# First channel attention of a six-stage kernel: band added by halves of 64 rows, rows normed in place and kept on chip, loads moved

## What is computed

```python
x = _layernorm(x + _L0_attn_ref(x, ...), axis=-1)
x = _layernorm(x + _L0_xattn_ref(x, ctx_2048, ..., 64), axis=-1)
x = _layernorm(x + _L0_ffn_ref(x, ...), axis=-1)
...
def _L0_xattn_ref(mask, encodings, w_in, b_in, w_out, b_out, w_ct, b_ct, local_size):
    N, E, T, H = (8, 64, 256, 8)
    ...
    scores = jnp.einsum('bqhd,bkhd->bhqk', q, k) / jnp.sqrt(jnp.asarray(d, q.dtype))
    idx = jnp.arange(t)
    band = jnp.abs(idx[:, None] - idx[None, :]) <= local_size
    scores = jnp.where(band[None, None], scores, neg)
    attn = jax.nn.softmax(scores, axis=-1)
    o = jnp.einsum('bhqk,bkhd->bqhd', attn, v).reshape(n, t, e)
    ...
    y = jax.nn.relu(o) * encodings
    out = jnp.einsum('nit,io->not', y, w_ct) + b_ct[None, :, None]
```

## Time and profile before

| | |
|---|---|
| median of 3 runs | 3762.48 us (3760.27 to 3763.68) |
| the profiled execution | 3755.11 us |
| its span | 3753.3 us |
| mean granted TensorE clock | 0.945 of full speed |
| TensorE busy | 3290.9 us, 88% |
| VectorE, ScalarE, POOL busy | 65%, 51%, 52% |
| stage_banded | about 384 to 725 us of the span |
| MLP | about 728 to 925 us |

### The profile page before, as it was taken

The page is one execution under the profiler, slowest core; times in us unless marked ns, Lnnn a source line. Parts: engine busy times, 40 slices in busy tenths (PEclk is TensorE's granted clock), DMA queues, the critical chain, the costliest instruction groups (busy, mean ns, idle before and its releaser), DMA issues. The chain is left out here.

```text
span 3753.3 us, 100900 instructions
## 1 busy us (share of the span) xinstructions
PE 3290.9 (88%) x37352; PEld 2245.7 (60%) x37352; DVE 2431.1 (65%) x4462; ACT 1923.2 (51%) x5120; POOL 1968.1 (52%) x2814
## 2 busy tenths in 40 slices
PE   9999599786899999999999999999998398779990
PEld 6777366464566666666666666666666255446550
DVE  5555366333677777777777777777777378534446
ACT  1111255422566666666666666666665177545550
POOL 2333333142556665665565655665565357657772
PEclk9999799897999999999999999999999599989995
DMA  2000544200221111111111111111110256366645
GB/s 80 11 11 8 132 115 115 70 1 18 56 57 49 40 47 47 48 40 49 46 49 40 52 45 50 44 53 37 57 56 23 65 144 175 113 209 208 213 155 208
DMA packets 229331, 285.18 MB, mean 76 GB/s; under 512 B 58756, under 2 KB 193352, under 8 KB 222184
## 3 DMA queue, kind: packets, MB, share of 16 engines
q1 hardware_dynamic: 210440, 243.87, 23.0%
q0 software_dynamic: 18432, 34.96, 2.7%
HBM read 166.39 MB, written 127.93 MB: 78 GB/s over the span
## 5 line engine op out<-in xcount | busy, mean ns | idle before, releaser
L2090 PE MATMUL head_ring<-gd_xT,head_w 128*128 128x512 f32 x1024 | 520.9, 633 | 15.4 <-DMA head_w<-gd_w 10.0
L2519 POOL TENSOR_TENSOR head_V<-head_V,gd_ones 128x512 bf16<-128x512 f32 x128 | 133.3, 1041 | 476.2 <-DVE head_V L2373 476.2
L1386 POOL DMA_INDIRECT ytok<-exp_y,exp_cur x256 | 252.5, 986 | 121.4 <-issue 72.7
L2348 DVE SCALAR_TENSOR_TENSOR head_cb_V<-head_ring,head_taps,head_cb_V 128x504 f32<-128x504 f32 (+2 forms) x384 | 279.8, 729 | 13.0 <-ACT head_cb_V L2233 8.4
L2090 PEld LDWEIGHTS head_ring<-gd_xT,head_w 128*128 128x128 f32 x1024 | 181.9, 198 | 154.6 <-issue 131.6
L2209 PE MATMUL head_by<-head_wo,head_ogT 128*128 128x256 f32 x1024 | 255.5, 393 | 9.4 <-issue 6.1
L2379 DVE TENSOR_TENSOR head_Xs<-head_bx,head_join 128x512 bf16<-128x512 f32 x320 | 219.8, 687 | 62.3 <-PE head_bx L2131 55.9
L2099 PE MATMUL head_ring<-head_w,gd_xT 128*128 128x256 f32 x1024 | 257.3, 394 | 2.8 <-DVE head_cb_V L2348 2.4
L2270 ACT CAST head_Tt<-head_btt 128x512 bf16<-128x512 f32 x320 | 191.3, 598 | 38.1 <-PE head_btt L2139 36.7
L2209 PEld LDWEIGHTS head_by<-head_wo,head_ogT 128*128 128x128 f32 x1024 | 185.1, 190 | 39.4 <-issue 14.4
L2099 PEld LDWEIGHTS head_ring<-head_w,gd_xT 128*128 128x128 f32 x1024 | 185.3, 191 | 35.5 <-DVE head_cb_V L2348 3.4
(11 more groups left out here) (345 smaller groups left out, 9064.3 us busy)
## 6 DMA issues: line engine op xcount, KB each, us to landing
xbuf<-head_blank SPq DMA_DIRECT2D x64, 552.0 KB
exp_xg<-xbuf SPq DMA_DIRECT2D x64, 552.0 KB, 5.2
head_gi<-scan SPq DMA_DIRECT2D x64, 256.0 KB
ytok<-head_blank SPq DMA_DIRECT2D x64, 256.0 KB
sum_yg<-ytok SPq DMA_DIRECT2D x16, 1024.0 KB, 7.0
moe_w<-moe_w SPq DMA_DIRECT2D x32, 384.0 KB, 3.2
cb_Q<-qd SPq DMA_DIRECT2D x48, 192.0 KB
cb_K<-kd SPq DMA_DIRECT2D x48, 192.0 KB
```

The costliest lines, as they stand in the source:

```text
L1386: pool.indirect_dma_start(ytok, bass.IndirectOffsetOnAxis(ap=cur[i % AHEAD][s][:, b:b + 1], axis=0), y[i % RESULTS][s][:, b, :], None, bou ...
L2090: last = pe.matmul(b[:, :], w[:, c, FEAT[what]], xT[:, c, n % UNITS * N:n % UNITS * N + N], start=c == 0, stop=c == DC - 1)
L2348: dve.scalar_tensor_tensor(out=out, in0=by_seq(bank_of(f, n))[:, :, 0:SEQ - s], scalar=taps[:, TAP[f], KS - 1 - s:KS - s], in1=out, op0=AL ...
```

## The change

- The band is added by four products in place of one: for each query block and each half of 64 rows, the two blocks of 64 keys where the band is not zero, from the identity's diagonal quarter. Blocks of the band that are wholly 0 are left out.
- The rows and ctxt of the stage live in `xc`, which is now made before the stage. The norm is written back over x in `xc`; `y`, the stores to x2, x2 itself and the MLP's loads of x are gone. The load of ctxt in the delta stage is gone too, with its semaphore.
- The identity is loaded once, into a tile that lives until the delta stage ends. The MLP's mixing and gate weights, gamma and offset are loaded during the channel attention, one at each of fetches 6 to 9, into tiles that are given back before the heads of the delta stage.
- Tile 2 of x and ctxt is loaded at the start of the stage; tiles 1 and 2 now stand ahead of the constants.
- On POOL the casts of the identity and the band come before `prefill()`, which moves behind the split of tile 1.

```diff
+            def bounds(pe, bank):
+                for i in range(QB):
+                    for side in range(2):
+                        rows = slice(side * SEQ, side * SEQ + SEQ)
+                        into, held = (t[rows, i * KW:i * KW + KW].rearrange("p (c k) -> p c k", k=SEQ) for t in (bank, band16))
+                        chunks = slice(1 - i, 3 - i) if side == i else slice(0, 3, 2)
+                        pe.matmul(into[:, chunks, :], ident16[rows, rows], held[:, chunks, :], start=i == 0, stop=False, skip_group_check=True)
...
-                        pe.matmul(b[:, 0:QB * KW], ident16[:, :], band16[:, :], start=True, stop=False, skip_group_check=True)
+                        bounds(pe, b)
...
-                        pe.matmul(b[:, 0:KB * KW], ident16[:, :], band16[:, :], start=True, stop=False, skip_group_check=True)
+                        bounds(pe, b)
...
                 load(0)
                 for t, name in early:
                     sp.dma_start(t, A[name]).then_inc(early_in, 16)
+                load(1)
+                load(2)
                 for t, name in loads:
                     sp.dma_start(t, A[name]).then_inc(weights_in, 16)
-                load(1)
...
-                        for ahead in range(2 if t == 0 else t + 3, min(t + 4, TILES)):
-                            load(ahead)
+                        if t + 3 < TILES:
+                            load(t + 3)
+                        if t >= 6 and t - 6 < len(early_weights):
+                            to, name = early_weights[t - 6]
+                            sp.dma_start(to, name).then_inc(next_in, 16)
...
-                        sp.dma_start(dst[t * P:t * P + P, :], y[u][:, :]).then_inc(stored[u], 16)
-                for u in range(2):
-                    sp.wait_ge(stored[u], START + TILES // 2 * 16)
+                sp.wait_ge(next_in, START + 16 * len(early_weights))
...
-                        if n >= 2:
-                            dve.wait_ge(stored[u], START + n // 2 * 16)
-                        norm_apply(dve, ln[u], [y[u][:, :]], [r[u][:, :]], [mv[u][:, :]], [rstd[u][:, :]], n // 2, 1)
+                        norm_apply(dve, ln[u], [x[:, n, :]], [r[u][:, :]], [mv[u][:, :]], [rstd[u][:, :]], n // 2, 1)
...
-                    pool.wait_ge(weights_in, START + 16 * len(loads))
-                    pool.tensor_copy(ident16[:, :], ident[:, :]).then_inc(bits_ready, 1)
-                    pool.tensor_copy(band16[:, :], band[:, :]).then_inc(bits_ready, 1)
...
                         if n == 0:
+                            pool.wait_ge(weights_in, START + 16 * len(loads))
+                            pool.tensor_copy(ident16[:, :], ident[:, :]).then_inc(bits_ready, 1)
+                            pool.tensor_copy(band16[:, :], band[:, :]).then_inc(bits_ready, 1)
+                        elif n == 1:
                             prefill()
...
-                    sp.dma_start(ident[:, :], A["ident"]).then_inc(weights_in, 16)
-                    load(0)
-                    sp.dma_start(wm[:, :, 0:D], A["expert_w"].rearrange("(c p) e -> p c e", p=P)).then_inc(mixed_in, 16)
-                    sp.dma_start(wm[:, :, D:D + E], A["mlp_gate"].rearrange("(c p) e -> p c e", p=P)).then_inc(mixed_in, 16)
                     sp.dma_start(wup[:, :, :], A["up_w"].rearrange("(c p) e -> p c e", p=P)).then_inc(up_in, 16)
-                    load(1)
                     sp.dma_start(wdown[:, :, :], A["down_w"].rearrange("(c p) e -> p c e", p=P)).then_inc(down_in, 16)
-                    sp.dma_start(offset[:, :], A["ln_beta"]).then_inc(offset_in, 16)
-                    sp.dma_start(gamma[:, :], A["ln_gamma"]).then_inc(gamma_in, 16)
-                    for s in range(2, UNITS):
-                        load(s)
...
-                    sp.dma_start(xc[:, :, 1, :], ctxt.rearrange("(t p) d -> p t d", p=P)).then_inc(ctxt_in, 16)
```

More of the change, by code:

```diff
@@ L1467, in _, with __init__, loads, rows @@
                         norm_rstd(pool, ln[u], [mv[u][:, :]], [var[u][:, :]], eps[:, :], power[:, :], [rstd[u][:, :]], t // SLOTS, 1)
-def stage_delta(nc, src, ctxt, xc, scan, xbuf, ytok, A):
+class MlpWeights:
+    def __init__(self, m):
+        self.wm = m.sb("wm", [P, DC, D + 8])
+        self.gamma, self.offset = m.sb("gamma", [P, D]), m.sb("offset", [P, D])
+    def loads(self, A):
+        def rows(name):
+            return A[name].rearrange("(c p) e -> p c e", p=P)
+        return [(self.wm[:, :, 0:D], rows("expert_w")), (self.wm[:, :, D:D + 8], rows("mlp_gate")),
+                (self.gamma[:, :], A["ln_gamma"]), (self.offset[:, :], A["ln_beta"])]
+class DeltaState:
+    def __init__(self, m):
+        self.ident, self.ones = m.sb("ident", [P, P]), m.sb("ones", [P, P])
+        self.power, self.root, self.eps, self.eps6 = (m.sb(n, [P, 1]) for n in ("power", "root", "eps", "eps6"))
+        self.shrink, self.per_dim, self.minus1 = m.sb("shrink", [P, 1]), m.sb("per_dim", [P, 1]), m.sb("minus1", [P, 1])
+        self.xT = m.sb("xT", [P, DC, ROWS])
+        self.beta, self.gsum = m.sb("beta", [P, TILES, 32]), m.sb("gsum", [P, TILES, 32])
+def stage_delta(nc, xc, state, weights, weights_held, scan, xbuf, ytok, A):
     NK, NV, DH, KS = 16, 32, P, 4
@@ L1510, in stage_delta @@
             IC, PAIR, HALF = I // P, range(2), TS // 2
-            wm, wup, wdown = m.sb("wm", [P, DC, D + E]), m.sb("wup", [P, DC, I]), m.sb("wdown", [P, IC, D])
-            gamma, offset = m.sb("gamma", [P, D]), m.sb("offset", [P, D])
+            wm, gamma, offset = weights.wm, weights.gamma, weights.offset
+            wup, wdown = m.sb("wup", [P, DC, I]), m.sb("wdown", [P, IC, D])
             wab, upto = m.sb("wab", [P, DC, 2 * NV]), m.sb("upto", [P, P])
             dt, alog, rate = (m.sb(n, [P, NV]) for n in ("dt", "alog", "rate"))
-            x = [m.sb(f"x{s}", [P, TS, D]) for s in range(UNITS)]
+            x = [xc[:, s * TS:s * TS + TS, 0, :] for s in range(UNITS)]
             xb, moe = ([m.sb(f"{n}{u}", [P, TS, D]) for u in PAIR] for n in ("xb", "moe"))
@@ L2648, in build @@
     stage_lightning(nc, x[0], x[1], A)
-    stage_banded(nc, x[1], x[2], A["ctxt"], qd, kd, A)
     with ExitStack() as ctx:
-        xc = Mem(nc, ctx, "rows").sb("xc", [P, TILES, 2, D])
-        stage_delta(nc, x[2], A["ctxt"], xc, scan, xbuf, ytok, A)
+        rows = Mem(nc, ctx, "rows")
+        xc = rows.sb("xc", [P, TILES, 2, D])
+        with ExitStack() as delta:
+            state = DeltaState(Mem(nc, delta, "gd"))
+            weights_held = delta.enter_context(ExitStack())
+            weights = MlpWeights(Mem(nc, weights_held, "ahead"))
+            stage_banded(nc, x[1], A["ctxt"], xc, state.ident, qd, kd, A, weights.loads(A))
+            stage_delta(nc, xc, state, weights, weights_held, scan, xbuf, ytok, A)
         stage_moe(nc, xc, out, qd, kd, xbuf, ytok, A)
```

42 lines of the change are left out of this document (13 added, 29 removed).

## The result

The changed kernel takes 3839.5 us (median of four runs, 3836.99 to 3877.0) against 3761.4 for the kernel before (four runs, 3756.88 to 3763.68). The ratio is 1.0232, with a 95% interval of 1.0169 to 1.0296. The kernel is slower by 78 us by the medians and by 87 us by the ratio, in which the one long execution of 3877.0 us counts; +51.5 was forecast, with 3840 us (+77.5) as the end of the range. The ratio lies beyond that end (1.0206), though its interval reaches over it. Where the executions of one kernel lie more than 1.5% apart, ratios here use the shorter ones alone. The profiled execution, the shortest of the four, took 3836.99 us; its span is 3835.2.

A forecast was written before the change was run, and what follows sets the result against it. The prediction took TensorE's queue to bound the middle of the channel attention, so each unit's added cost shows 1 to 1. Halves +71, start -10 and seam -9.5 gave +51.5 us, 3814 us in all, range 3790 to 3840.

The forecast's parts named there:

- Part 1, the price of a block: Band products in the channel attention: a block by halves takes 0.33 us against 0.167, +0.163 us a unit.
- Part 1, the full clock: Middle of the channel attention: all 456 blocks costed at full clock, +74.3 us; sum of the part +71 us.
- The clock: Rival: many gaps lower the granted clock in the channel attention, some 30 us more, 3845 us; chance 0.07.
- Part 2, the start: Start of the channel attention: third tile's earlier load brings the second pass near 428 instead of 438.4, -10 us.
- its first half: Start of the channel attention: the first unit can start at about 408.5 us, 10 us earlier.
- The rival that the start gains nothing: Start of the channel attention: transfers of the first two tiles set it, +10, 3824 us; no chance of its own.
- Part 3, the seam: From channel attention to MLP: without the last store and reload, the first up-product comes near 735.5 instead of 744.84, -9.5 us.
- The sum: Whole kernel: 71 - 10 - 9.5 = +51.5 us, added to the median of 3762.5, gives 3814 us.

The follow-up runs named there:

- four_full: The changed kernel with the band added by four products of 96 columns on the full array: 3891.52 against 3910.68 us for the kernel before, ratio 0.9951.
- two_blocks_together: The changed kernel with the first pass's blocks of two units issued one behind the other: 3944.02 against 3901.18 us for the kernel before, ratio 1.0108.
- after_again: The changed kernel, unaltered, run again on a chip of the experiments: 3974 to 4026 us in four runs, ratio 1.0206 to the kernel before.
- whole_at_start: The changed kernel with whole products in the first 100 blocks and halves from there on: 3950.9 against 3910.68 us for the kernel before, ratio 1.0106.
- one_product: The changed kernel with the band added by one product of 384 columns again: 3892.24 against 3910.68 us for the kernel before, ratio 0.9944.
- place_first: The changed kernel with one product for the band and the spreads three steps later: 3886.69 against 3901.18 us for the kernel before, ratio 0.9959.
- one_third_late: The changed kernel with one product for the band and the third tile's load in its old place: 3880.65 against 3901.18 us for the kernel before, ratio 0.9957.
- late_and_place: The changed kernel with one product, the third tile's load in its old place and spreads three steps later: 3889.04 against 3907.89 us for the kernel before, ratio 0.9955.
- before_again: The kernel before, unaltered, profiled again on a chip of the experiments: 3898.08 us in its profiled execution.
- one_pair: The changed kernel with only two of each block's four products: 4022.0 to 4139.7 us, ratio 1.034 to the kernel before by the two shorter runs.

## Why the prediction was wrong

**Part 1, the price of a block: right.** 0.24 and 0.26 us between the starts, 22.85 us a tile against 22.7, 61 to 63 us for 412 blocks against 62. That the price is the change of shape is shown from both sides: four products without one cost 0.007 us a block (four_full), and taking two of a pair's four changes away gives 0.21 us of the expected 0.22 (two_blocks_together). Both agree with what the Trainium skill states (TensorEngine Tiling, Key Properties), that changing the tiling mode, not just the tile, drains TensorE; its price here is 0.09 us.

**Part 1, the full clock: this step failed.** The sum of +74.3 us took all 456 blocks at full clock, since the middle of the stage before has it. The clock stood among the rivals, with 0.07 and as a matter of gaps in the middle. What happens is something else: the clock is at its lower level when both passes begin, and the halves keep it there. It cost 87.5 - 71 = 16.5 us in the first profile and, by the same sum, 61 us in that of after_again. The length of the lower level accounts for both: a tile takes 37.87 us at it and 22.85 at the full one, so a microsecond at the lower level loses 0.40; the 40.5 us from 441.3 to 481.8 lose 16, the 153.8 us from 437.3 to 591.1 lose 61. The cost disappears when the first 100 blocks are whole. The evidence I weighed against this rival, 0.98 with as many changes of shape in another stage, was read in a stretch that enters at full clock (1.00 from 1000 to 1040 us); it says that a high clock can survive such work, as whole_at_start confirms from 442.8 us on, and nothing on whether a low one recovers under it. That a high one always survives is not so either: the changed kernel lost it at 430.6 us, 3.5 us after it had come.

**Part 2, the start: this step failed.** Forecast -10, measured -0.3 for the second pass (-8.6 for the first, as its first half said). The rival that the start gains nothing was the true one in its time, and in part in its cause. The sum put the arrival of the second tile's gather at 417 to 418 us, since "that wave has passed" behind 408. But in the kernel before the DMA share is 0.76 to 1.10 again in every 2 us from 412 to 424, and the units that need this gather start at 428.63 us in the changed kernel (425.5 on the clock of the kernel before) and at 425.61 in one_product. I followed the first band product, which is not what the end hangs on: the second pass hangs on the second tile's gather and on the copy of the maxima, and SP issues that copy 50.8 and 50.9 us after the stage's first load, before and after. That these two set it together is argued from the order of the queues; place_first, with the copy 6.6 us sooner and the pass only 3.4, says that the copy alone does not. I had named the gather, and not followed what SP issues between it and the copy. With the early load taken away (one_third_late) the second pass starts 51.9 us after the first load against 53.9 with it, so the load gives this start nothing; in the order of place_first, where the copy comes sooner, taking it away goes with a start 4.8 us later (55.3 against 50.5), and no whole time shows either.

**Part 3, the seam: right.** -10.7 against -9.5, and every profile with the change's seam has it: 20.6 to 22.3 us from the last value products to the first up-product, against 32.0 to 33.2 in the three profiles with the old one. On one of the experiments' chips the up-product comes 361.4 us after the stage's first load in the kernel before and 351.4 in late_and_place; on the other it comes 351.7 us after it in one_product.

**The sum.** +3.1 ahead of the stage, -0.3, +87.5, -10.7 and +2.2 behind it are the 81.9 us between the spans. Two terms failed, the start by 9.7 us and the first part by the clock's 16.5, both in the same direction. The 3.1 us ahead of the stage and the 2.2 behind it are no larger than what single executions differ by.

**What stays open.** Up to the first up-product one_product is 9.7 us shorter than the kernel before (before_again, on the other of the two chips), and the whole kernel 22 us (15 to 29). The 12 us between are not found: behind the first up-product, single executions of these kernels differ by 10 us and more from each other. Nor is it known why the clock comes back at 481.8 us in one execution and at 591.1 in another of the same program, on another chip, nor which property of the short blocks holds it down: the changes of shape, the part of the array that stands idle and the fewer columns are not told apart by these runs.

**The best version** is one product with the rest of the change: 0.9944 of the time of the kernel before (0.9926 to 0.9962). four_full, one_third_late, place_first and late_and_place cannot be told from it.

## What to carry to other kernels

Cost a change of the array's shape (the part of it that a product uses) by itself, 0.09 us each way here, and put blocks on parts of the array next to each other. Such a block between full products loses when the columns that it saves are worth less than its two changes; by 0.18 us and 0.43 ns a column that is an estimate of some 420 columns, and the block here saved 128. Before costing a change at full clock, look at the level at which its stage begins, since work that can keep a high clock need not bring a low one back. And follow an early start through to the last pass that depends on it: the queue that issues the later steps in program order may not have moved.

## What the runs showed of the hardware

- The clock's recovery hangs on the kind of work, not on whether the queue is full. Once both passes run it is at full level from 439.2 to 444.1 us into the span with a block on the whole array (eight profiles, four_full with its four products among them), with halves in one pass from 445.5, with two blocks together from 474.9, with all halves from 481.8, 486.3 and 591.1, and with one pair from 885.8, while the records have TensorE busy for 120 of 120 us (480 to 600).
- Fewer instructions can be slower for that reason alone: 34.46 us a tile with two products in a block, until 885.8 us in the profiled execution, against 22.85 with four once the clock is up; at the lower level the four need 37.87.
- The changed kernel scatters more: 3974 to 4026 us in four runs, against 3893 to 3922 in sixteen of the kernel before beside it, and its runs line up by their mean granted clock (0.927 down to 0.917).
- Products on diagonal quarters of one bank run side by side: in the profiles of the changed kernel and of one_pair the two of a pair start 0 to 4 ns apart.
- Products of 96 columns on the whole array, each with its own weight load, cost hardly more in a row than one of 384: 18.16 against 17.95 us a tile of 32 blocks.
